# A shorter lead of the first attention in a ring of softmax tiles

## The chip, the cores and the metric

One core of a Trainium2 chip runs the kernel. The metric is the device time in microseconds; the kernel was run several times, and the median counts. TensorE (PE) multiplies matrices, VectorE (DVE) and ScalarE (ACT) do the elementwise work and empty the accumulation banks, GpSimd (POOL) takes a few elementwise steps, and SyncE (SP) issues the DMAs.

## The reference, cut to what matters

A batch of 16 graphs with 512 nodes and 256 features passes through four layers, all in float32. Each ends in a residual and a norm over the features.

```python
x = layernorm(x + (norm_adj @ (x @ W0) + b0))                     # layer 0
x = layernorm(x + o + ln(o)),   o = softmax(mask(q k^T)) v @ Wproj # layer 1: attention, 8 heads of 32
for _ in range(3):                                                # layer 2: a gated recurrence
    a = adj @ h
    z = sigmoid(W3 [a, a] + U3 h);  r = sigmoid(W4 [a, a] + U3 h)
    h = (1 - z) * h + z * tanh(W5 [a, a] + U5 (r * h))
x = layernorm(x + h)
x = layernorm(x + softmax(q k^T / sqrt(32) + bias(adj)) v @ Wo)     # layer 3: attention, 8 heads of 32
```

Within a batch everything is one chain. Between batches nothing depends on anything.

## The kernel before, in words

Three batches are in flight, each in buffers of its own (`STREAMS = 3`, batch b uses set b % 3). The matrix products are split into a high and a low part and made with three matmuls each (`product`, L1451 to L1453). Every product lands in one of eight accumulation banks, from which ScalarE takes the high part and VectorE the rest.

Both attentions share one ring of softmax tiles. An attention of one batch (a block) is 32 tiles of 128 queries by 512 keys. A tile is one matmul for the scores (L1500), a masked maximum on VectorE (L1224), the exponential on ScalarE (L990), four transposes on TensorE (L1508) and a copy on either engine (L999, L1235). After every eight tiles comes the product with the values (L1523) and a rescaling (L1528, L1004, L1245, L1012, L884). The queries and keys of four heads are copied into one buffer, `stack`, by twelve DMAs (L823), which wait until the earlier tiles of that head have been read. The ring is strictly in order. Its order is `BLOCKS`: the pair (1, b) is the first attention of batch b, here called A(b), and (3, b) is the second, C(b). Before the change it is

A(0) A(1) A(2) C(0) A(3) C(1) A(4) C(2) ... A(15) C(13) C(14) C(15).

Around it each batch has work that is not in the ring. Ahead of A(b) lie the load, scaling, adjacency product, first weights, a norm, transposes (L1491) and q, k, v. Between A(b) and C(b) lie a projection, two norms, three recurrent steps (each with an adjacency product, gates, and transposes of the state, L1561), and q, k, v again. Behind C(b) come a projection, a norm and the store (L804). Batch b + 3 can be loaded (L800) only when batch b has been stored.

The order of all instructions on all engines is made when the kernel is built. `Order` holds the pieces of work in queues, each with an estimated duration and the pieces it waits for, and runs them through a list scheduler: the piece that can start first goes first, and among those that can start at once the one with the longest way to the end. The table `RANK` adds a number in microseconds to that way, by kind of piece. The result is a fixed instruction list for each engine.

```python
late = TO_PE if piece.engines == ("PE",) else 0.0
...
rank = (start, -way[piece.key], took(piece, e))
```

One row buffer holds in turn the row to be added before the first layer (`scale`), `beta` and `bo`; the order of these loads, `ROWS`, is fixed and not changed.

Of the kernel before, what the change touches and what calls it, by code (L numbers as in the profile page):

```python
# [15 lines left out]
STREAMS = 3  # L16
# [60 lines left out]
def nominal(key):  # L77
# [21 lines left out]
    else:  # L99
# [3 lines left out]

RANK = {"act a": 6.5, "act ax": 3, "act hT": 6.5, "act hf": -5.5, "act k": 0.5, "act n0": -8, "act n1": -4,
        "act n3": -4, "act out0": 0.5, "act out2": 0.5, "act q": -7, "act r": -8, "act rh": 13, "act rows2": -12,
        "act state": 4, "act x3T": 8, "act z": 4, "act zt": 1, "dve a": 1, "dve h": -12, "dve hT": 0.5,
        "dve norm_o": 4.5, "dve out1": -1, "dve proj1": 1, "dve proj3": 6, "dve q": -6, "dve res2": -2,
        "dve rh": -13, "dve rows2": -1, "dve scale": 3, "dve w0": -3, "dve x1T": -8, "dve x2T": -2, "dve x3T": -2.5,  # L110
        "first ax 1": -100, "first ax 2": 298, "first beta": 200, "first k": 3, "first load": 300, "first q": 33,
        "first scale 0": -10, "first scale 1": -3, "first scale 2": 0.5, "first v": -12, "first w0 0": 301,
# [3 lines left out]
        "pool oadd": 2, "pool out3": 0.5, "pool rstd": 3.5, "pool scale": -4, "prep adj0": 100, "prep adj2": -100,  # L116
        "prep bo": 10, "prep deg": -30, "prep dinv": 3, "prep hi_k3": 2, "prep hi_o1": 3, "prep hi_o3": -1.5,
        "prep hi_v3": 10, "prep lo_k3": -1, "prep lo_o1": 7, "prep lo_qkv1": -300, "prep lo_u5": 10,
        "prep lo_w3": -10, "prep mask1": -0.5, "prep mask3": -300, "prep q1": -110, "prep w4": 110,
        "prep w4-w3": -30, "prep w5": 308, "prep warm": 300, "pt": -2, "raw": 1.5, "recip": -2.5, "row": -0.5}  # L120


FIRST = ("scale", "ax", "w0", "n0", "rstd", "x1T", "q", "k", "v", "beta")
# [2 lines left out]
def kind_of(key):  # L126

    kind, what = key[:2]
    if kind == "prep":
        return f"prep {key[2]}"  # L130
    if kind in ("pe", "act", "dve", "pool"):
        b = key[2]
        if what in FIRST and b < STREAMS and (what not in ("q", "k", "v") or key[3] == 1) and (
                what != "rstd" or key[3] == "n0"):
            return f"first {what} {b}" if what in ("scale", "ax", "w0") else f"first {what}"
        return f"{kind} {what}"
    if kind == "load" and what < STREAMS:
        return "first load"
    return f"values {key[2]}" if kind == "values" else kind
# [11 lines left out]
class Order:  # L151
# [31 lines left out]
    def run(self):  # L183
        way = {key: us + RANK.get(kind_of(key), 0.0) for key, us in self.ways().items()}
        done, taken = {}, {}
# [43 lines left out]
def adj_resnorm_kernel(nc, x, adj, w0, b0, wqkv, wproj, bproj, gamma, beta, w3, w3b, u3, u3b, w4, w4b,  # L229
                       w5, w5b, u5, u5b, wq, bq, wk, bk, wv, bv, wo, bo, out):  # L230
    B, N, D = x.shape
# [15 lines left out]
    bs = range(B)  # L247


    BLOCKS = [(1, b) for b in bs if b < STREAMS]  # L250
    for b in bs:
        BLOCKS += [(3, b)] + ([(1, b + STREAMS)] if b + STREAMS < B else [])
    block_at = {block: i for i, block in enumerate(BLOCKS)}


# [6 lines left out]
    def tile_of(t):  # L262

        i, r = divmod(t, TILES)
        gh, r = divmod(r, GROUP)
        h, q = divmod(r, QT)
        return *BLOCKS[i], gh // HALVES, gh % HALVES, h, q

# [61 lines left out]
    for b in bs:  # L330
        j = b % STREAMS
        pe, act, dve, pool, sp = ((e, j) for e in ("pe", "act", "dve", "pool", "sp"))
# [23 lines left out]
        for layer in (1, 3):  # L356
# [75 lines left out]
            row = "beta" if layer == 1 else "bo"  # L432
            add(pool, "POOL", ("pool", row, b), ("dve",) + xT + (FT - 1,), ("row", row_at[row, b]))
            for g in range(G):
# [4 lines left out]
                first = (block_at[layer, b] * TILES + g * HALVES * GROUP)  # L439
# [16 lines left out]

    for t in range(len(BLOCKS) * TILES):
        layer, b, g, half, h, q = tile_of(t)
# [35 lines left out]
    with ExitStack() as ctx:  # L494
        def sb(name, shape, dt=F32):
            return ctx.enter_context(nc.sbuf_tensor(name, shape, dt))

        def sem(name):
            return ctx.enter_context(nc.semaphore(name))
# [6 lines left out]
        mask1 = sb("mask1", [P, NT, N], BF16)  # L506
        mask3 = sb("mask3", [P, NT, N])
# [6 lines left out]
        def of_few(n):  # L514
            nonlocal taken
            taken += n
            return few[:, taken - n:taken]

        cols = of_few(5 * FT).rearrange("p (i f) -> p i f", i=5)
        dinv, power, least, one, spare = (of_few(n) for n in (NT, NT, P_RING, 1, SPARE))  # L520
# [23 lines left out]
        stack = sb("stack", [P, 2, HG, N], F32R)  # L544
# [7 lines left out]
        rsum = o32[:, :].rearrange("p (q c) -> p q c", q=QT)  # L552
# [11 lines left out]
        raw = nc.alloc_sbuf_tensor_at("raw", [P, FT, PLAIN], F32, offset=at)  # L564
# [9 lines left out]
        deg = probs[:, 2, 0:3 * NT].rearrange("p (i t) -> p i t", i=3)  # L574
# [41 lines left out]
        def signals(name, steps):  # L616
            return [Signal(sem(f"{name}{j}"), steps) for j in js]
# [21 lines left out]
        state = signals("state", ["x2_0", "x2_1"])  # L639
# [7 lines left out]
        summed = signals("summed", [f"{n}{t}" for n in ("n0", "n1", "n2", "n3") for t in range(NT)])  # L647
        ALL = range(len(BLOCKS) * TILES)
        groups = range(len(BLOCKS) * GROUPS)
        shifted = Signal(sem("shifted"), ALL)  # L650
# [993 lines left out]
```

How the kernel before makes its waits and increments, by code:

```python
        def wait_free(pe, *name):  # L695
            uses = order.on_bank[order.banks[name]]
            n = uses.index(name)
            if n and uses[n - 1] != ("warm", 0):
                sig, value = last_read(*uses[n - 1])
                pe.wait_ge(sig.sem, value)
# [11 lines left out]
        def wait_full(eng, *name):  # L714
            bank_full = full[order.banks[name]]
            eng.wait_ge(bank_full.sem, bank_full.at(name))
# [1 line left out]
        def wait_sig(eng, sig, step, b):  # L719
            eng.wait_ge(sig.sem, sig.at(step, b // STREAMS))
# [1 line left out]
        def wait_pt(eng, t):  # L722
            for sig, mine in ((pt_act, moved["ACT"]), (pt_dve, moved["DVE"])):
                last = max([u for u in mine if u <= t], default=None)
                if last is not None:
                    eng.wait_ge(sig.sem, sig.at(last))
# [24 lines left out]
            def raw_loads(what):  # L752
# [12 lines left out]
                        sp.dma_start(to, w.rearrange("(o p) c -> p o c", p=P)).then_inc(gru_loaded, 16)  # L765
                elif what == "rows":
                    for i, v in enumerate((gamma, bproj)):
                        sp.dma_start(rows[:, 1 + i, :], v.partition_broadcast(P)).then_inc(rows_loaded, 16)
                elif what == "bo_sum":
                    sp.wait_ge(prep_dve.sem, prep_dve.at("bo"))
                    sp.dma_start(bo_sum[:, :], raw_bo[0:1, :]).then_inc(bo_stored, 16)
                else:
# [64 lines left out]
            def bias_columns():  # L837
                pool.wait_ge(rows_loaded, 16 * 2)
                pool.wait_ge(small_loaded, SMALL)
```

## Time and profile before

| | us |
|---|---|
| median of 3 runs | 2557.17 |
| lowest and highest | 2555.69, 2558.51 |
| span of the profiled execution | 2555.1 |
| TensorE busy in it | 2518.8 |
| ScalarE busy | 1935.7 |
| VectorE busy | 1872.5 |
| GpSimd busy | 757.7 |

The span runs from the first to the last instruction of one profiled execution; for that execution no time of its own is given beside the span, so it is set against the median, which lies 2.1 us above. Busy time is the time in which an engine had an instruction in work. The ends of matmuls are modelled, so a busy TensorE is not yet a TensorE at its peak.

### The profile page before, as it was taken

What the parts mean: (1) busy time and instruction counts of PE and PEld (TensorE: products, weight loads), DVE (VectorE), ACT (ScalarE), POOL (GpSimd) and SP (SyncE); (2) the same over time, 40 slices, a digit from 0 to 9 for tenths busy, and PEclk for the clock granted to TensorE, in tenths of its full rate; (3) what the DMA queues carried; (4) which work ended last, traced back from release to release, by engine and by line L of the source; (5) the groups of instructions that cost most, each with busy time, mean ns of one, the idle gap of its engine ahead of it and who ended that gap; (6) DMA issues with size and microseconds to landing.
All of it is one profiled execution on the core that took longest, in us unless ns stands there. A gap on an engine that the chain in (4) does not pass through costs nothing.

```text
span 2555.1 us, 50270 instructions
## 1 busy us (share of the span) xinstructions
PE 2518.8 (99%) x17401; PEld 2043.1 (80%) x17401; DVE 1872.5 (73%) x5440; ACT 1935.7 (76%) x4388; POOL 757.7 (30%) x1083
## 2 busy tenths in 40 slices
PE   8999999999999999999999999999999999999997
PEld 6777787888878888888888888888888888778875
DVE  8858848778686786867768587685877868666776
ACT  5858849678596886959869597785968869675787
POOL 2223332323224232242332324232232322423222
PEclk9999999999999999999999999999999999999999
DMA  5302113022130312203122131221303123021122
GB/s 145 78 19 59 26 46 71 26 61 45 46 77 20 76 30 59 65 21 77 43 54 53 41 70 32 54 51 46 78 19 67 38 54 70 20 52 27 28 54 69
DMA packets 91083, 132.15 MB, mean 52 GB/s; under 512 B 15921, under 2 KB 40146, under 8 KB 90834
## 3 DMA queue, kind: packets, MB, share of 16 engines
q1 hardware_dynamic: 90834, 128.94, 21.4%
q8 instruction: 143, 2.34, 0.4%
q14 instruction: 106, 0.87, 0.1%
HBM read 19.83 MB, written 8.39 MB: 11 GB/s over the span
## 4 chain that ended last, share of the span: by engine, by line
PE 91%; ACT 3%; DVE 3%; issue 1%; SPq 1%; POOL 1%; DMA 0%; ACTq 0%; POOLq 0%; DVEq 0%
PE bank L1451 18%; PE bank L1453 18%; PE bank L1452 18%; PE bank L1508 16%; PE bank L1523 9%; PE bank L1500 8%; PE bank L1528 2%; PE bank L1491 2%; PE bank L1561 1%; ACT probs L990 1%; ACT PT L999 1%; DVE gate L1209 0%; ACT res L1027 0%; SPq L749 0%; DVE probs L1224 0%
## 5 line engine op out<-in xcount | busy, mean ns | idle before, releaser
L990 ACT ACTIVATE probs<-probs,few 128x512 f32<-128x512 f32 x1024 | 732.0, 722 | 38.9 <-DVE few L1224 36.5
L1224 DVE CUSTOM_DVE_ANT_0 probs<-bank,mask 128x512 f32<-128x512 f32 x1024 | 675.4, 685 | 111.8 <-PE bank L1508 65.2
L1508 PE MATMUL bank<-ident,probs 128*128 128x128 f32 x4096 | 580.5, 273 | 7.0 <-ACT probs L990 5.9
L1508 PEld LDWEIGHTS bank<-ident,probs 128*128 128x128 f32 x4096 | 485.4, 141 | 76.6 <-issue 10.3
L999 ACT ACTIVATE PT<-bank 128x512 f32<-128x512 f32 x672 | 377.7, 594 | 51.9 <-PE bank L1528 42.8
L1500 PE MATMUL bank<-stack 96*128 96x512 f32 x1024 | 411.6, 450 | 1.0 <-DVE few L1224 0.8
L1235 DVE COPY PT<-bank 128x512 f32<-128x512 f32 x352 | 240.7, 687 | 69.5 <-PE bank L1528 48.2
L1451 PE MATMUL bank<-feat,W 128*128 128x512 f32 x640 | 258.6, 404 | 0.0
L884 POOL TENSOR_TENSOR feat<-o,feat 128x256 fp32r<-128x256 f32 x128 | 95.2, 743 | 542.0 <-ACT feat L1012 541.5
L1453 PE MATMUL bank<-feat,W 128*128 128x512 f32 x640 | 252.7, 395 | 0.0
L1452 PE MATMUL bank<-feat,W 128*128 128x512 f32 x640 | 252.7, 395 | 0.0
L1523 PE MATMUL bank<-PT,vh 128*32 128x256 f32 x4096 | 250.5, 382 | 0.3 <-DVE few L1224 0.3
L1451 PE MATMUL bank<-qk,W 128*128 128x512 f32 x576 | 231.8, 402 | 0.0
L1453 PE MATMUL bank<-qk,W 128*128 128x512 f32 x576 | 227.5, 395 | 0.0
L1452 PE MATMUL bank<-qk,W 128*128 128x512 f32 x576 | 227.4, 395 | 0.0
L1027 ACT ACTIVATE res<-res,few 128x256 f32<-128x256 f32 x256 | 139.7, 595 | 95.0 <-POOL few L869 92.8
L1451 PE MATMUL bank<-adjT,qk 128*128 128x512 f32 x512 | 204.6, 400 | 5.3 <-DVE qk L1374 2.4
L911 POOL TENSOR_TENSOR o<-sums,few 128x256 f32<-128x256 f32 x128 | 82.2, 642 | 412.0 <-DVE sums L1240 411.6
L1523 PEld LDWEIGHTS bank<-PT,vh 128*32 128x32 f32 x4096 | 118.6, 109 | 106.0 <-issue 35.9
L1452 PE MATMUL bank<-adjT,qk 128*128 128x512 f32 x512 | 202.4, 395 | 0.0
L1453 PE MATMUL bank<-adjT,qk 128*128 128x512 f32 x512 | 202.0, 395 | 0.0
L990 ACT ACTIVATION_READ_ACCUMULATOR probs<-probs,few 128x1 f32 x1024 | 201.8, 197 | 0.0
(113 smaller groups left out, 4972.7 us busy)
## 6 DMA issues: line engine op xcount, KB each, us to landing
stack<-qk SPq DMA_DIRECT2D x768, 128.0 KB, 2.4
res<-in_x_dram SPq DMA_DIRECT2D x16, 512.0 KB, 3.8
out_dram<-res SPq DMA_DIRECT2D x16, 512.0 KB, 3.0
rows<-bo_sum SPq DMA_DIRECT2D x15, 128.0 KB, 2.9
rows<-in_L_gnn_bias_dram SPq DMA_DIRECT2D x14, 128.0 KB, 2.9
rows<-in_L_gnn_ln_beta_dram SPq DMA_DIRECT2D x14, 128.0 KB, 2.9
PT<-in_adj_dram SPq DMA_DIRECT2D x1, 1024.0 KB, 5.3
vh<-in_L_gnn_w_w_dram SPq DMA_DIRECT2D x2, 512.0 KB, 9.3
```

The source lines that it names most:

```text
L884: i = pool.tensor_tensor(feat[j][:, LO, gh // HALVES, sl], o32[:, :], feat[j][:, HI, gh // HALVES, sl].bitcast(F32), ALU.subtract)
L990: k = act.activation(p, p, ACT.Exp, bias=least[:, t % P_RING:t % P_RING + 1], scale=-1.0, accum_out=sums[:, grp % 2, q * HG + h:q * HG + h ...
L999: k = act.activation(PT[:, t % PT_RING, :], place("transpose", t)[:, :], ACT.Copy)
L1027: k = act.activation(res[j][:, t, :], res[j][:, t, :], ACT.Identity, bias=mv[j][:, t, 0:1], scale=mv[j][:, t, 1:2])
L1224: k = dve.tensor_tensor_reduce(out=probs[:, t % P_RING, :], in0=place("scores", t)[:, :], in1=mask[:, half * QT + q, :], scale=1.0, scalar ...
L1235: k = dve.tensor_copy(PT[:, t % PT_RING, :], place("transpose", t)[:, :])
L1451: pe.matmul(dst, a(HI), b(LO), start=start, stop=False)
L1452: pe.matmul(dst, a(HI), b(HI), start=False, stop=False)
L1453: return pe.matmul(dst, a(LO), b(HI), start=False, stop=stop)
L1500: k = pe.matmul(place("scores", t)[:, :], stack[0:STACKED * HD, 0, h, cs], stack[0:STACKED * HD, 1, h, :], start=True, stop=True)
L1508: k = pe.transpose(place("transpose", t)[:, m * P:(m + 1) * P], probs[:, t % P_RING, m * P:(m + 1) * P], ident[:, :])
L1523: pe.matmul(dst[h * HD:(h + 1) * HD, 0:QH], v_v[j][:, m, c:c + HD], pt_v[:, pt_slots(grp, h), m, :], start=(m == 0), stop=(m == NT - 1))
```

## The change

The lead of the first attention falls from three batches to two: `BLOCKS` starts with A(0) A(1), and A(b + 2) follows C(b). The ring becomes

A(0) A(1) C(0) A(2) C(1) A(3) C(2) ... C(13) A(15) C(14) C(15).

The number of buffer sets stays three. The `RANK` table is replaced as a whole by another one with more entries; all else is the same. The diff, with the two tables cut:

```diff
-RANK = {"act a": 6.5, "act ax": 3, "act hT": 6.5, "act hf": -5.5, "act k": 0.5, "act n0": -8, "act n1": -4,
...
-        "pe hT": 20, "pe proj1": -3.5, "pe q": 0.5, "pe r": -0.5, "pe v": 3.5, "pe w0": 5, "pe x1T": -1.5,
...
+RANK = {"act ax": 80.53, "act c": 10.01, "act hT": 5.52, "act hf": -0.19, "act k": 2.4, "act n0": -11.72,
...
+        "pe cw": 4, "pe hT": 118.66, "pe k": -0.65, "pe proj1": 1.49, "pe proj3": -51.87, "pe q": -0.97, "pe r": -1.23,
+        "pe v": 3.24, "pe w0": 9.96, "pe x1T": 16.3, "pe x2T": -5.31, "pe x3T": 49.73, "pe z": 6.71, "pe zu": 2.75,
...
@@ -247,9 +255,10 @@
-    BLOCKS = [(1, b) for b in bs if b < STREAMS]
+    LEAD = STREAMS - 1
+    BLOCKS = [(1, b) for b in bs if b < LEAD]
     for b in bs:
-        BLOCKS += [(3, b)] + ([(1, b + STREAMS)] if b + STREAMS < B else [])
+        BLOCKS += [(3, b)] + ([(1, b + LEAD)] if b + LEAD < B else [])
```

## Rows read from the trace of the kernel before

**Rows 1.** The page: span, busy times of TensorE and weight loads, granted clock.

```profile
span 2555.1 us, 50270 instructions
...
PE 2518.8 (99%) x17401; PEld 2043.1 (80%) x17401; DVE 1872.5 (73%) x5440; ACT 1935.7 (76%) x4388; POOL 757.7 (30%) x1083
...
PEclk9999999999999999999999999999999999999999
```

**Rows 2.** Windows of one period: length, busy (x instructions) by engine, clock, DMA.

```profile
844.30:1000.00 155.70, 155.70 (x1085) 127.24 (x1084) 114.49 (x337) 120.44 (x275) 47.47 (x68) 1.00 0.22 51
1000.00:1155.70 155.70, 155.70 (x1085) 127.24 (x1084) 114.51 (x337) 120.44 (x275) 47.47 (x68) 1.00 0.22 51
```

**Rows 3.** Timeline of TensorE, undisturbed matmuls: start us, us, what.

```profile
647.70 0.40 PE L1451 MATMUL bank<-adjT,qk 128*128 128x512 f32 x1
...
650.27 0.40 PE L1453 MATMUL bank<-feat,W 128*128 128x512 f32 x1
...
2494.55 0.28 PE L1451 MATMUL bank<-W,feat 128*128 128x256 f32 x1
...
2495.85 0.28 PE L1453 MATMUL bank<-W,feat 128*128 128x256 f32 x1
```

**Rows 4.** Groups by line and shape: count, busy us, mean ns, idle before.

```profile
L1508 PE MATMUL bank<-ident,probs 128*128 128x128 f32 x4096 | 580.5, 273 | 7.0 <-ACT probs L990 5.9 <-ACT PT L999 0.3
...
L1451 PE MATMUL bank<-feat,W 128*128 128x512 f32 x640 | 258.6, 404 | 0.0
```

**Rows 5.** Timeline of TensorE: first and last tiles of blocks, state transposes.

```profile
93.42 0.48 PE L1500 MATMUL bank<-stack 96*128 96x512 f32 x1
...
221.41 1.04 PE L1561 MATMUL bank<-ident,vh 128*128 128x128 f32 x8
...
251.15 0.48 PE L1500 MATMUL bank<-stack 96*128 96x512 f32 x1
...
2284.54 0.71 PE L1500 MATMUL bank<-stack 96*128 96x512 f32 x2
...
2494.24 0.48 PE L1500 MATMUL bank<-stack 96*128 96x512 f32 x1
```

**Rows 6.** The chain that ended last: start us, us, piece.

```profile
549.19 1.86 PE bank L1523 x32
```

**Rows 7.** Windows of five stretches that make up the span.

```profile
0.00:40.00 40.00, 28.49 (x151) 24.12 (x152) 28.86 (x58) 21.70 (x40) 5.93 (x22) 0.96 0.62 188
40.00:400.00 360.00, 352.57 (x2396) 282.27 (x2395) 264.64 (x770) 264.06 (x600) 102.30 (x145) 1.00 0.22 49
400.00:2160.00 1760.00, 1759.95 (x12306) 1436.83 (x12305) 1296.04 (x3818) 1370.91 (x3127) 534.72 (x753) 1.00 0.22 51
2160.00:2500.00 340.00, 337.41 (x2185) 271.02 (x2184) 247.08 (x671) 240.26 (x528) 103.20 (x138) 1.00 0.17 41
2500.00:2555.10 55.10, 40.33 (x370) 28.87 (x368) 35.90 (x126) 38.76 (x98) 11.54 (x26) 0.97 0.19 49
```

**Rows 8.** Windows of one period's two parts: ring stopped, ring running.

```profile
621.40:688.50 67.10, 67.10 (x361) 55.06 (x360) 39.01 (x110) 36.40 (x70) 27.53 (x41) 1.00 0.12 33
688.50:777.00 88.50, 88.50 (x726) 72.14 (x725) 75.40 (x227) 83.95 (x206) 19.93 (x27) 1.00 0.29 65
```

**Rows 9.** Timeline of SyncE's queue between C(3) and A(6).

```profile
801.49 0.40 SPq L804 DMA_DIRECT2D out_dram<-res  x1
804.45 0.39 SPq L800 DMA_DIRECT2D res<-in_x_dram  x1
...
838.87 31.78 SPq L823 DMA_DIRECT2D stack<-qk  x24
```

**Rows 10.** Timeline of SyncE's queue near the end.

```profile
2464.45 27.48 SPq L823 DMA_DIRECT2D stack<-qk  x15
2491.97 0.59 SPq L804 DMA_DIRECT2D out_dram<-res  x1
```

More of the change, by code:

```diff
@@ L101, in nominal @@
     return us, LATE[kind]
-RANK = {"act a": 6.5, "act ax": 3, "act hT": 6.5, "act hf": -5.5, "act k": 0.5, "act n0": -8, "act n1": -4,
[L107 to L112, printed above, removed]
[3 rows of a table removed]
[L116 to L120, printed above, removed]
@@ new lines @@
+RANK = {"act ax": 80.53, "act c": 10.01, "act hT": 5.52, "act hf": -0.19, "act k": 2.4, "act n0": -11.72,
+        "act n1": 26.1, "act n2": 1.88, "act n3": -27.67, "act out0": 1.14, "act out2": 0.5, "act q": -18.92,
+        "act r": 5.4, "act rh": -9.54, "act rows2": 12.64, "act scale": -0.21, "act state": -5.81, "act v": 5.6,
+        "act x1T": 5.97, "act x2T": 2.67, "act x3T": 1.55, "act z": 1.36, "act zt": -14.35, "dve a": 8.23,
+        "dve ax": -0.46, "dve b0": 16.03, "dve h": -14.81, "dve hT": 4.98, "dve k": -30.26, "dve mom_o": 10.49,
+        "dve out1": -1.32, "dve proj1": 26.19, "dve proj3": -0.12, "dve q": 14.8, "dve r": -15.19, "dve res2": -1.03,
+        "dve rh": -1.94, "dve rows2": 299.23, "dve scale": 0.86, "dve w0": -64.59, "dve x1T": -0.49, "dve x2T": -0.47,
+        "dve x3T": -2.78, "exp": -0.82, "first ax 0": 4.53, "first ax 1": 0.41, "first ax 2": -1.68, "first beta": 0.5,
+        "first k": -3.16, "first load": -1.87, "first n0": -17.72, "first q": -3.4, "first rstd": 204.33,
+        "first scale 0": -8.87, "first scale 1": -7.77, "first scale 2": 8.51, "first v": -24, "first w0 0": 4.76,
[3 rows of a table added]
+        "pool beta": -20.25, "pool bo": 1.74, "pool hf": -25.07, "pool oadd": -1.43, "pool out3": -491.55,
+        "pool rh": 188.64, "pool rstd": 276.57, "pool scale": 241.79, "prep adj0": -31.1, "prep adj1": -23.61,
+        "prep adj3": 6.65, "prep bo": 2.82, "prep cols": 46.18, "prep deg": 214.04, "prep dinv": 12.04,
[3 rows of a table added]
+        "prep lo_w0": 0.73, "prep mask1": 0.88, "prep mask3": 16.77, "prep pow": -27.3, "prep q1": 4.3,
+        "prep q3": 2.94, "prep u3": -19.58, "prep u5": -53.35, "prep w3": 3.79, "prep w4": -4.86, "prep w4-w3": 25.81,
+        "prep w5": 13.69, "prep warm": -15.96, "pt": -2, "raw": 5.98, "recip": -5.82, "row": -0.08, "rsum": 118.21,
+        "stack": -16.09, "store": 1.05, "stt": 0.43, "values 0": 236.49, "values 1": 5.38}
```

6 rows, old and new, of the table RANK are left out of this document.

## Prediction

> **What bounds the kernel now.** I read the page first: TensorE is busy for 99% of the span, and the granted clock is full throughout [rows 1]; VectorE and ScalarE are busy for about three quarters [rows 2]. A busy TensorE need not be a full one, since the ends of its matmuls are modelled, so the second view is the cadence. Where nothing interrupts, the 512-column matmul starts every 0.2336 us (eleven steps in 2.57 us) and the 256-column one every 0.118 us (eleven in 1.30 us) [rows 3]. Eight transposes that last 1.04 us, each 0.273 us long, start (1.04 - 0.273) / 7 = 0.110 us apart [rows 4, 5], and the 32 matmuls of a values group take 1.86 us of the chain [rows 6].
>
> With the counts this gives TensorE's work for one of the 16 batches. There are 5184 matmuls with 512 columns outside the ring (nine groups, 640, 576 and 512 times three), so 324 x 0.2336 = 75.7; 1920 with 256 columns (three groups of 640), so 120 x 0.118 = 14.2; 64 scores x 0.2336 = 14.9; transposes (4096 of the ring and 1024 others) 320 x 0.109 = 34.9; eight values groups x 1.86 = 14.9, and about 0.15 each for entering and leaving that shape = 1.2. The sum is 155.8 us.
>
> The third view is the period. Two successive stretches of 155.7 us hold the same 1085 matmuls, and the busy times of every engine repeat within 0.1 us [rows 2]. So in the middle the kernel is TensorE's work and nothing else: 155.7 measured against 155.8 summed. VectorE takes 114.5 and ScalarE 120.4 of each period.
>
> What is left is at the two ends. 16 x 155.7 = 2491.2, and the span is 2555.1: 63.9 us. TensorE is idle for 11.5 in the first 40 us and for 14.8 in the last 55, for 7.4 and 2.6 in the stretches beside these, and for 0.05 in the 1760 us between [rows 7]. The rest is preparation (up to 10 us of matmuls, nearly all in the first 40 us) and waits so short that the modelled ends cover them. I take 63.9 - 10 - 11.5 - 14.8 = about 27 us as what an order of the work could still win, all of it between 40 and 400 us and after 2160 us. The first 11.5 are loads and preparation, and the last 14.8 the tiles of the last block, which alternate between engines, and the closing norm and store.
>
> **The change, part by part.** No instruction is added or removed: the ring still has 1024 tiles. What changes is which tiles neighbour each other.
>
> *The middle.* Call A(b) the first attention of batch b and C(b) its second. Before, A(b + 3) stands straight behind C(b), in the same buffers, so the ring stops while the output of b is projected and stored, batch b + 3 loaded and its first matmuls made: 67.1 us per period in which TensorE runs full on the recurrent steps (361 matmuls, 67.10 busy of 67.10) [rows 8]. The store, load and stack DMAs show this chain: store at 801.5, load at 804.5, stack from 838.9 [rows 9]. After, two blocks stand between C(b) and A(b + 3), so this chain is covered. The stop was costing nothing, for TensorE was full in it; removing it gains 0, because the 155.7 us of TensorE's work remain.
>
> The price is a shorter cover for the other chain, from A(b) to C(b), with three recurrent steps. Before, four blocks and two stops lay over it; after, two blocks. Its shortest passage in this trace is batch 0: the first tile of A(1), 93.4, to the first of C(0), 251.2: 158 us [rows 5]. The ring's own pace is some 42 us a block (88.5 us for two with their neighbours [rows 8]). In the new order a period lasts at least half of (this chain plus two blocks): (158 + 85) / 2 = 122 us. That is below 155.7, so TensorE stays the bound until the chain has grown to 226 us. Both ends: 0 if it stays below, and for each 10 us beyond, 5 us a period over some 13 periods. I take 0, since the traffic that lengthens the chain is matmul work that has to be done anyway.
>
> *The start.* Until C(0) can begin, the new order has only A(1) to run in the ring. A block costs TensorE 32 x (0.2336 + 4 x 0.109) + 4 x 2.2 = 30.3 us; the work between A and C is 155.7 - 60.6 - 17.7 (adjacency, first weights, q, k, v) - 2.8 (last projection) = 74.6. Over the 158 us there are A(1) with 30.3, batch 0 with 74.6, and batch 1 from 133 us on, 118 / 158 of 74.6 = 55: 160 us, just enough and with no reserve. Before, A(2) was in reserve too. Bounds: a gain up to the 7.4 us that the busy time shows idle here [rows 7] and the hidden part, a loss of as much.
>
> *The end.* The new ring closes A(15), C(14), C(15), the old one A(15), C(13), C(14), C(15). The chain from A(15)'s last tile (2284.5) to C(15)'s first (2494.2) took 210 us before [rows 5], with two blocks over it. If it shrinks to 158, the filling is C(14) with 30.3, batch 15 with 74.6, two projections with 5.7, and what is left of batch 14: that must be 48 us or more of its 74.6. If it is, nothing is lost; if 20 are left, 28 us stand idle.
>
> *The ranks.* They decide ties between ready pieces, on all queues, the preparation included. They can't touch the middle's sum, only the 27 us. I take about a third of those, 8 us: more seems too much, with fewer streams to fill the ends from, and less too little, since the old start is visibly loose [rows 7].
>
> *SyncE's queue.* Before, store and load fell into the ring's stop, where no stack copy was due [rows 9]. After, they stand among the stack copies of A(b + 2), on one queue, in order; a store that waits for the last norm holds them up. The only place of the old trace with this crossing is the tail, 15 stack copies over 27.5 us and a store behind them [rows 10]; in the 340 us that hold it TensorE is idle for 2.6 [rows 7]. From both sides: 0, or 1 us a period. I take 0, and keep 13 us for the range.
>
> The sum: 2555.1 + 0 (middle) - 8 (ends) = 2547.1. The median lies 2.1 us above the span, so **2549 us**.
>
> One rule of the Trainium skill speaks for far more (Perfetto Trace Analysis, "Optimization Strategy" and "Identifying the Most-Contended Engine"): where the contended engine changes between regimes, interleaving them can help, and TensorE's headroom is to be judged by LDWEIGHTS busy and not by matmul busy. Here LDWEIGHTS is busy for 80% [rows 1], which by that rule would leave a fifth; the rows on the cadence disagree.
>
> **The rivals.**
> 1. *The ends come out even*: what the ranks win, the thinner filling takes. 2552 to 2562, 2557.
> 2. *The ends get longer (the other side)*: less than 40 us of batch 14 is left when A(15) ends, or the 160 us at the start don't mesh. Price: some 20 us of the tail's 28, less the ranks' 8, so 12 more: 2569. For it: the filling was computed at no reserve. Against it: the planner prefers the longest way, so it puts off batch 14 for A(15).
> 3. *The queue or the chain costs something in every period*: 1 us x 13 = 13: 2570; a chain of 240 us instead of 226 would cost 7 x 13 = 91: 2648, which I leave outside.
> 4. *TensorE is not full in the ring's stretch*, and spreading the ring shortens the period: 5 us of hidden waiting in 88.5 would give 13 x 5 = 65, so 2492. For it: ScalarE is busy for 84 of these 88.5 us and for 36 of the stop's 67.1 [rows 8]. Against it: the cadence sum leaves no 5 us. This is what the skill's rule would make of it.
>
> **How the numbers follow.** Forecast 0.41, even 0.25, longer ends 0.19, every period 0.12, TensorE not full 0.03. The measurement can tell 0.2%, 5 us, from no change. Faster: 0.41 + 0.03 = 0.44; same 0.25; slower 0.19 + 0.12 = 0.31. The range goes from 2535 (22 of the 27 us won) to 2580 (the longer ends at their full 28 us, less some of the 8); the forecast case alone spans 2537 to 2552.
>
> **What would show it.** Right: periods in the middle of 155.7 us again, with TensorE full and with the scores spread over them; C(0) near 250 us; an idle sum outside the middle that is 8 us lower. Wrong: a middle period of over 156.5 us, waits of the scores for the stack copies, or over 15 us idle between the end of A(15) and C(15).

## The result, and the profile after

The change made the kernel slower: a median of 2615.66 us (2615.04 to 2616.76, 4 runs) against 2556.48 before (2555.69 to 2558.51, now 4 runs too), a ratio of 1.0232 with a 95% interval of 1.0217 to 1.0246. That is 59 us more. The forecast was 2549, and the range ended at 2580.

The page of the changed kernel: span, busy times, the chain by engine.

```profile
span 2614.9 us, 50087 instructions
...
PE 2546.4 (97%) x17401; PEld 2055.3 (79%) x17401; DVE 1900.9 (73%) x5457; ACT 1951.7 (75%) x4385; POOL 747.1 (29%) x1083
...
PE 84%; DVE 8%; ACT 3%; POOL 2%; issue 1%; SPq 1%; DMA 0%; DVEq 0%; ACTq 0%; POOLq 0%
```

Against [rows 1] TensorE makes the same 17401 matmuls in 27.6 us more of busy time and stands idle for 68.5 us where it was 36.3. Part of the longer busy time is the granted clock: it is at its lower level for 45 us in all, against 7 us before. By the pace of the rows at the end of this document (0.213 us instead of 0.117 between two matmuls) that is 17 us of the 59 at most, an estimate. (All line numbers after are higher by nine: the scores are L1509, the ring's transposes L1517.)

Windows of the changed kernel: the first 40 us, the stretch to the first tile of C(2), the ten periods from there to the first tile of C(12), the end.

```profile
0.00:40.00 40.00, 23.86 (x117) 19.19 (x118) 28.49 (x56) 21.72 (x40) 7.37 (x22) 0.89 0.60 188
40.00:570.40 530.40, 517.68 (x3441) 419.24 (x3440) 380.79 (x1086) 378.91 (x844) 149.24 (x217) 0.98 0.19 44
570.40:2164.40 1594.00, 1573.56 (x10842) 1272.90 (x10841) 1173.32 (x3379) 1214.07 (x2734) 469.92 (x671) 1.00 0.21 50
2164.40:2614.90 450.50, 431.29 (x3007) 343.97 (x3005) 318.31 (x939) 336.97 (x771) 120.58 (x175) 0.99 0.21 48
```

The middle is where the time went. Ten periods took 1594.0 us, 159.4 each, against 155.7 in [rows 2], with 20.4 us of idle TensorE where [rows 7] show 0.05 in 1760. That is 37 us in ten of the sixteen periods; of the 17 that are not idle time some 3 are the clock's, by the estimate above, and the rest is in waits that the modelled ends of matmuls cover, which no view separates. The rest of the 59 came ahead of this stretch and behind it; the first 40 us alone lose 4.6 us more than before.

The ring still stops, but once in two batches: four blocks, then a stop. Timeline of TensorE, the scores that open C(2), close A(4) and open C(4); then windows of the four blocks and of the stop behind them.

```profile
570.45 0.94 PE L1509 MATMUL bank<-stack 96*128 96x512 f32 x3
...
689.50 0.48 PE L1509 MATMUL bank<-stack 96*128 96x512 f32 x1
...
888.67 0.94 PE L1509 MATMUL bank<-stack 96*128 96x512 f32 x3
```

```profile
570.30:818.70 248.40, 246.37 (x1798) 198.63 (x1797) 184.59 (x552) 203.69 (x475) 65.34 (x86) 1.00 0.24 55
818.70:888.60 69.90, 67.79 (x375) 55.43 (x375) 49.69 (x126) 39.48 (x75) 28.82 (x49) 1.00 0.13 33
```

C(2) opens at 570.4, A(4) ends at 689.5, and C(4) opens at 888.7: two blocks take 119 us, the chain from A(4) to C(4) 199, and together they are the 318 us of two periods. In the stop TensorE idles for 2.1 us, and in the four blocks ahead of it for 2.0; in [rows 8] it did in neither. The longest waits of TensorE in the ten periods (us in total, times, longest):

```profile
PE bank L1500 <- ACT res L1036: 8.0, 15, 1.2
PE bank L1532 <- DVE PT L1244: 4.1, 5, 0.8
PE bank L1517 <- ACT probs L999: 3.8, 5, 0.8
```

The first is in the stop, the other two belong to the ring's own tiles and make up as much. I followed the first; its timeline, of TensorE first:

```profile
852.22 0.73 PE L1500 MATMUL bank<-ident,res 128*128 128x128 f32 x2 [0.26 <-ACT res L1036]
854.12 0.33 PE L1500 MATMUL bank<-ident,res 128*128 128x128 f32 x1 [1.18 <-ACT res L1036]
854.62 0.77 PE L1500 MATMUL bank<-ident,res 128*128 128x128 f32 x5 [0.16 <-ACT res L1036]
```

These are the transposes x2T of batch 5. They wait for the last norm behind the first attention, and everything behind them in TensorE's fixed list waits too. Why that norm is late is seen on VectorE and GpSimd, a few us earlier:

```profile
841.26 3.00 POOL L885 TENSOR_TENSOR res<-res,vh 128x512 f32<-128x512 f32 x2
841.41 3.40 DVE L1335 SCALAR_TENSOR_TENSOR gate<-gate,vh 128x512 f32<-128x512 f32 x2
844.22 3.18 POOL L910 TENSOR_TENSOR feat<-gate,feat 128x512 fp32r<-128x512 f32 x2
844.73 2.95 DVE L1309 SCALAR_TENSOR_TENSOR vh<-vh,few,rows 128x256 f32<-128x256 f32 x2
```

The two operations of L1335 take 1.7 us each where their group's median is 0.68, the two of L1309 1.5 instead of 0.48. In the whole trace 13 of the 96 operations of L1335 and 29 of the 64 of L1309 are lengthened by over 15%, each while GpSimd works on SBUF. Groups of the changed kernel:

```profile
L1335 DVE SCALAR_TENSOR_TENSOR gate<-gate,vh 128x512 f32<-128x512 f32 x96 | 77.5, 819 | 4.8 <-ACT gate L1060 4.8
...
L1309 DVE SCALAR_TENSOR_TENSOR vh<-vh,few,rows 128x256 f32<-128x256 f32 x64 | 52.8, 864 | 6.2 <-POOL res L885 6.2
```

The same two lines before, L1326 and L1300, took 708 and 522 ns on average, so (819 - 708) x 96 + (864 - 522) x 64 = 33 us of VectorE's time are new. The list scheduler has no such lengthening in its durations.

### The profile page after: what moved, and what is told of

It reads as the page before. It is cut to its first block, busy times and chain, and to the rows that moved or that the text cites. A ratio compares the mean times of both kernels' runs of the same rounds, so it can differ in the third digit from the quotient of the medians.

```text
span 2614.9 us, 50087 instructions
## 1 busy us (share of the span) xinstructions
PE 2546.4 (97%) x17401; PEld 2055.3 (79%) x17401; DVE 1900.9 (73%) x5457; ACT 1951.7 (75%) x4385; POOL 747.1 (29%) x1083
## 4 chain that ended last, share of the span: by engine, by line
PE 84%; DVE 8%; ACT 3%; POOL 2%; issue 1%; SPq 1%; DMA 0%; DVEq 0%; ACTq 0%; POOLq 0%
PE bank L1460 16%; PE bank L1462 16%; PE bank L1461 16%; PE bank L1517 15%; PE bank L1532 8%; PE bank L1509 8%; DVE vh L1309 2%; PE bank L1537 2%; PE bank L1500 1%; PE bank L1570 1%; DVE gate L1218 1%; ACT probs L999 1%; DVE probs L1233 1%; ACT res L1036 1%; POOL few L870 1%
## 5 line engine op out<-in xcount | busy, mean ns | idle before, releaser
L1517 PE MATMUL bank<-ident,probs 128*128 128x128 f32 x4096 | 590.8, 273 | 19.5 <-ACT probs L999 15.3
L1517 PEld LDWEIGHTS bank<-ident,probs 128*128 128x128 f32 x4096 | 489.9, 141 | 103.5 <-issue 22.3
L1509 PE MATMUL bank<-stack 96*128 96x512 f32 x1024 | 431.9, 460 | 2.9 <-DVE few L1233 1.6
L1008 ACT ACTIVATE PT<-bank 128x512 f32<-128x512 f32 x669 | 384.7, 598 | 63.8 <-PE bank L1517 31.8
L1532 PE MATMUL bank<-PT,vh 128*32 128x256 f32 x4096 | 250.0, 382 | 4.4 <-DVE PT L1244 4.3
L1532 PEld LDWEIGHTS bank<-PT,vh 128*32 128x32 f32 x4096 | 119.5, 109 | 110.8 <-issue 36.8
L910 POOL TENSOR_TENSOR feat<-gate,feat 128x512 fp32r<-128x512 f32 x96 | 127.2, 1340 | 237.1 <-ACT feat L1064 237.1
```

Of the source, the lines that this page charges most:

```text
L910: i = pool.tensor_tensor(feat[j][:, LO, f, :], src[j][:, f, :], feat[j][:, HI, f, :].bitcast(F32), ALU.subtract)
L1008: k = act.activation(PT[:, t % PT_RING, :], place("transpose", t)[:, :], ACT.Copy)
L1509: k = pe.matmul(place("scores", t)[:, :], stack[0:STACKED * HD, 0, h, cs], stack[0:STACKED * HD, 1, h, :], start=True, stop=True)
L1517: k = pe.transpose(place("transpose", t)[:, m * P:(m + 1) * P], probs[:, t % P_RING, m * P:(m + 1) * P], ident[:, :])
L1532: pe.matmul(dst[h * HD:(h + 1) * HD, 0:QH], v_v[j][:, m, c:c + HD], pt_v[:, pt_slots(grp, h), m, :], start=(m == 0), stop=(m == NT - 1))
```

## The experiments

Twelve kernels, each timed beside the kernel before on the same chip. (The changed kernel was not timed again; the kernel before repeats within 0.5 us from chip to chip.) Two theories stood at first: the ring's order costs the time, or the new rank table does.

**The order alone**, with the old table:

```diff
-RANK = {"act ax": 80.53, "act c": 10.01, ...
+RANK = {"act a": 6.5, "act ax": 3, ...
```

> The new ring order with the old rank table. Theory O (the order costs the time: the chain from A(b) to C(b) has two blocks over it instead of four, so that in the ring's stops too little matmul work is ready): at least as slow as the changed kernel, 2610 to 2660 us, with TensorE idle in every period of the middle. Theory R (the new ranks cost the time): back near 2557 us, 2550 to 2570.

Measured 2737.98 us, ratio 1.0707 (1.0691 to 1.0723). Two periods of the middle take 337.7 us. The largest single wait comes six times, 36.6 us in all: w0 of a coming batch (here 8) stands in TensorE's list where its input isn't ready. One row of the timeline:

```profile
1219.21 0.55 PE L1452 MATMUL bank<-W,feat 128*128 128x256 f32 x1 [6.10 <-DVE feat L1200]
```

**The table alone**, on the old order:

```diff
-    BLOCKS = [(1, b) for b in bs if b < LEAD]
+    BLOCKS = [(1, b) for b in bs if b < STREAMS]
```

> The old ring order with the new rank table. Theory O: middle periods stay near 155.7 us with TensorE full; only the start keeps the 8 us that the changed kernel lost in its first 40 us, so 2560 to 2575 us. Theory R: 2600 us or more, with the middle period near 159 us.

Measured 2622.13 us, 1.0256 (1.024 to 1.0271), with middle periods of 159.6 us:

```profile
873.70:1033.30 159.60, 157.86 (x1087) 127.57 (x1086) 119.42 (x344) 119.10 (x272) 47.42 (x67) 1.00 0.21 50
```

So each half of the change is slow with the other half missing, and neither theory stands as put: theory R named this time and period but failed on the first kernel; theory O held there, beyond its range, and failed here. With the new table a period takes about 159.5 us in either order; with the old table it takes 155.7 in the old order and 168.9 in the new. These two kernels don't say, then, what the order costs with a good table of its own. That question stayed for the last pair.

**One piece later in TensorE's list:**

```diff
+    for b in bs:
+        late = [("pe", "x2T", b, f) for f in range(FT)]
+        i = line.index(late[0])
+        if line[i:i + 4] == late + [("pe", "w0", b + 1, tp) for tp in range(NT // 2)]:
+            line[i:i + 4] = line[i + 2:i + 4] + late
```

> The changed kernel, but on TensorE alone the two x2T pieces of every second batch stand behind the two w0 pieces of the next batch instead of ahead of them (six places). Theory O: the adjacency product behind them waits for rows2 all the same, at the end of the same chain of norms, so the idle time only moves: within 4 us of the changed kernel. Rival P (a bad place of one piece in TensorE's list): the wait of 2.6 us disappears in six places, and three drops of the clock with it: 12 to 20 us faster.

Measured 2615.33 us (2611.1 to 2616.55), as before the edit. The wait moved to w0 and to the adjacency product behind it:

```profile
851.74 0.36 PE L1467 MATMUL bank<-W,feat 128*128 128x256 f32 x1 [1.95 <-DVE feat L1215]
...
856.43 0.47 PE L1467 MATMUL bank<-adjT,qk 128*128 128x512 f32 x1 [0.77 <-DVE qk L1328]
```

At 852 us neither of the two pieces next in the list was ready: the list runs short of ready work there, and exchanging them doesn't mend that.

**GpSimd's addition cut** to 8 of 256 columns, all lists as they are:

```diff
-                i = pool.tensor_tensor(res[j][:, sl, :], res[j][:, sl, :], v_v[j][:, sl, :], ALU.add)
+                i = pool.tensor_tensor(res[j][:, sl, 0:8], res[j][:, sl, 0:8], v_v[j][:, sl, 0:8], ALU.add)
```

> The changed kernel, with GpSimd's addition of the attention output (L885) cut to 8 of 256 columns, so that most of the first attention's residual is left out of the sum. Orders of all engines stay. If VectorE's operations are stretched because GpSimd works on SBUF beside them, the two operations of norm_o that start with it (L1309) fall from 0.86 us on average to under 0.7, x2T comes 1.5 to 2.5 us earlier in every second period, and 8 to 18 us are won. If they are long for another reason: L1309 stays at 0.86 us and the time within 5 us.

Measured 2588.19 us, 1.0124 (1.0107 to 1.014): 27 us of the 59 are gone, more than expected. L1335 is back at its median, L1309 fell to 730 ns, not under 700: 20 of its 64 operations are still lengthened, most of them by L910. TensorE's waits for x2T in ten periods fall from 8.0 us to 0.8, its idle time there from 20.4 to 9.7. It is also at the lower clock for 21 us in all instead of 45; by the same estimate, up to 11 of the 27 us are the clock's. Window of two periods, now 315.2 us:

```profile
561.30:876.50 315.20, 313.36 (x2172) 253.94 (x2170) 231.30 (x676) 243.44 (x549) 89.64 (x135) 1.00 0.22 50
```

**The addition moved to VectorE**, nothing left out:

```diff
+            pools.remove(("pool", "oadd", b, tp))
+            line.insert(line.index(("dve", "mom_o", b, tp)) + 1, ("dve", "oadd", b, tp))
...
-                i = pool.tensor_tensor(res[j][:, sl, :], res[j][:, sl, :], v_v[j][:, sl, :], ALU.add)
+                i = dve.tensor_tensor(res[j][:, sl, :], res[j][:, sl, :], v_v[j][:, sl, :], ALU.add)
```

> The changed kernel with the addition of the attention output (32 instructions of 1.4 us on GpSimd, L885) moved to VectorE behind the moments of the same rows; all other pieces keep their places in every engine's list. Theory G (GpSimd's work beside VectorE stretches VectorE's operations and the chain of norms with them): VectorE gets 32 x 0.7 = 22 us more work and still the kernel is 8 to 25 us faster than the changed one, 2590 to 2607 us, and the stretched L1309 falls below 0.75 us. Rival V (VectorE's load decides, and the earlier gain came from work left out): no faster than 2612 us.

Measured 2599.65 us, 1.0167 (1.0152 to 1.0183): 16 us faster than the changed kernel, with more work on VectorE. L1309 (L1313 here) is at 630 ns. The same move in the kernel before:

> The same move in the kernel before, whose lists hardly let GpSimd's operations meet VectorE's (the operations in question take 0.52 us there, against 0.86). Theory G: nothing to win, within 4 us of 2557. If the move is good in itself, whatever the order: 8 us or more faster.

Measured 2556.83 us, 0.9998 (0.9989 to 1.0007), no difference. In the kernel before, where few operations were lengthened, the move is worth nothing.

**Both of GpSimd's operations cut**, the addition and the low part of the state:

```diff
-                i = pool.tensor_tensor(feat[j][:, LO, f, :], src[j][:, f, :], feat[j][:, HI, f, :].bitcast(F32),
-                                       ALU.subtract)
+                i = pool.tensor_tensor(feat[j][:, LO, f, 0:8], src[j][:, f, 0:8], feat[j][:, HI, f, 0:8].bitcast(F32),
+                                       ALU.subtract)
```

> The changed kernel with two of GpSimd's operations cut to 8 columns, the addition of the attention output and the low part of the recurrent state (L910), so that most of the first attention's residual and most low parts of the recurrence are left out. It shows what the order costs without any meeting of the two engines. Theory G alone: the middle period returns to 155.7 to 156.3 us and the time to 2565 to 2575. Theory G plus O (the order also leaves too little ready work when the ring's copies wait behind norm work on VectorE and ScalarE): a middle period of 157 us or more and 2575 to 2590.

Measured 2580.17 us, 1.0092 (1.0075 to 1.0109). L1309 is at 533 ns, as in the kernel before, and GpSimd has 13 us less per period to do; still two periods take 313.8 us, 156.9 each, and not 155.7. No wait for x2T is left in ten of these periods; the 4.1 us in which TensorE waits for copies of the ring's tiles (L1532) are there as before.

```profile
557.70:871.50 313.80, 312.67 (x2172) 253.85 (x2169) 229.28 (x676) 243.00 (x548) 68.12 (x135) 1.00 0.22 51
```

**The start.** The old table's entries for preparation and first pieces in the new table:

> The changed kernel with the old rank table's entries for the preparation and the first pieces (all names that begin with prep, first or raw), the rest of the table new. If the preparation's order costs the 8 us that TensorE lost in its first 40 us: 12 to 14 us idle there instead of 21.5, and the kernel 5 to 10 us faster, 2606 to 2611, as long as what follows isn't upset by the shift. If the rank entries are only good together: no faster, or slower.

Measured 2614.24 us, 1.0223 (1.0208 to 1.0238). TensorE is busy for 29.54 us of the first 40 instead of 23.86, and no more than 1.4 us of it reach the end, less than the two medians can tell apart; 5 to 10 were expected:

```profile
0.00:40.00 40.00, 29.54 (x154) 25.21 (x155) 29.23 (x59) 22.26 (x42) 6.21 (x22) 0.96 0.60 188
```

**GpSimd's addition three times over**, in both kernels, to see which of them bears a longer chain:

```diff
-                i = pool.tensor_tensor(res[j][:, sl, :], res[j][:, sl, :], v_v[j][:, sl, :], ALU.add)
+                for op, name in ((ALU.add, "a"), (ALU.subtract, "b"), (ALU.add, "c")):
+                    i = pool.tensor_tensor(res[j][:, sl, :], res[j][:, sl, :], v_v[j][:, sl, :], op)
```

> The kernel before, with GpSimd's addition of the attention output done as add, subtract, add in turn (5.6 us more of GpSimd per batch, and as much longer a chain of norms). Theory C (what makes the new order slow is that the chain from A(b) to C(b) has no slack left, so that each stretch of it reaches TensorE): here four blocks lie over the chain, and the cost is at most 1 us a batch, 2557 to 2573 us. Rival (meetings of VectorE and GpSimd cost TensorE time wherever they stand): 2 us a batch or more, over 2589.

> The same in the changed kernel. Theory C: most of the 5.6 us of each batch and of the meetings it adds reach TensorE, which waits in its fixed order: 3 to 7 us a batch, 2665 to 2730 us. Rival: as much as in the kernel before, whatever that is.

Measured 2623.62 us (1.0263, 1.0248 to 1.0279) in the kernel before and 2692.28 (1.0528, 1.0511 to 1.0546) in the changed one: 67 and 77 us more. The expectation for the kernel before was wrong, the one for the changed kernel held. But the longest wait on TensorE in the kernel before, in the waits by engine and line (us in total, times, longest), is not for the norms:

```profile
PE bank L1533 <- POOL o L916: 27.8, 13, 3.7
```

L916 is the ring's own small GpSimd operation, queued behind the longer additions, and TensorE's values group waits for it. The clock is at its lower level more often as well. The pair lengthened a queue that the ring needs, not only the chain, so it doesn't tell the two apart.

**Both orders with the same treatment.** The planner was told of the meetings, and a random search over the ranks, from each order's own table, minimised the planned span; the old order was given less time for it.

```diff
             clock[e] = start + took(piece, e)
+            if piece.key[1] in MET and e == "DVE":
+                clock[e] += min(MET[piece.key[1]], 0.65 * max(0.0, clock.get("POOL", 0.0) - start))
```

> The new ring order. The planner adds up to 2.0 us to norm_o and up to 1.1 us to rh on VectorE when GpSimd is at work as they start, and the ranks were searched again with that. If the loss came from meetings that the planner didn't know of: 20 to 35 us faster than the changed kernel, 2580 to 2595, with L1309's mean under 0.7 us or its length allowed for. If a better table can bring the order to the old time: under 2565. If the plan's own idle time and the start weigh as much as the meetings: 2590 to 2605.

> The old ring order with the same planner, ranks searched in the same way from the old table, for less time. If the order of the ring is what leaves too little ready work: near the kernel before or a little faster, 2545 to 2562 us, and 25 us or more faster than the new order with the same treatment. If the treatment decides and not the order: within 10 us of it.

Measured: the new order 2615.25 us (1.0236, 1.0219 to 1.0253), the old order 2556.36 (1.0002, 0.9993 to 1.0011). The treatment gave neither of them anything, and the 59 us between the orders stayed; for the new order none of the three expectations came true, the old order came out as its first one had it. The useful part is the traces. Groups of the kernel with the old order, the lines that stand for L1335 and L1309 and one that was hardly stretched before, L1326; then one of its periods:

```profile
L1326 DVE SCALAR_TENSOR_TENSOR gate<-gate 128x512 f32<-128x512 f32 x96 | 93.0, 969 | 3.3
L1317 DVE SCALAR_TENSOR_TENSOR gate<-gate,vh 128x512 f32<-128x512 f32 x96 | 69.0, 733 | 6.0 <-ACT gate L1042 6.0
...
L1291 DVE SCALAR_TENSOR_TENSOR vh<-vh,few,rows 128x256 f32<-128x256 f32 x64 | 35.1, 589 | 8.3 <-POOL res L867 8.3
```

```profile
844.70:1000.50 155.80, 155.80 (x1085) 127.64 (x1084) 120.22 (x342) 119.02 (x270) 47.19 (x68) 1.00 0.22 51
```

VectorE is busy for 120.2 us of this period, 5.7 more than in [rows 2], and TensorE is full all the same. Of the 5.7, 3.4 are five more copies of ring tiles, which VectorE took over from ScalarE, and 2.9 are lengthened operations (2.4 of them L1326; other lines are a little shorter). Over the whole kernel the lengthening sums to 48 us here, to 40 in the changed kernel and to 8 in the kernel before. So as much of it as the new order has costs the old order nothing, though it falls on other operations: most of it on the gates of the recurrence here, most on the norm behind the first attention there. In the new order, searched again, L1309 (L1292 there) still takes 964 ns, and TensorE waits 19.0 us in six places for a low part from GpSimd:

```profile
PE bank L1443 <- POOL feat L893: 19.0, 6, 3.2
```

## Why the prediction was wrong, step by step

**What bounds the kernel** was right: the cadence sum gave 155.8 us of matmul work per batch, and the best any run reached is 155.7 to 155.8. A faster period, rival 4, never appeared.

**The middle is the step that failed**: "I take 0, since the traffic that lengthens the chain is matmul work that has to be done anyway". The term of the middle was 0 and measured 3.7 us a period: TensorE does wait there, 2.0 us a period by the idle time alone, and not for matmul work but for norms and tile copies of VectorE and ScalarE that come late in its fixed list. The relation that I tested it with could not have shown this. Its terms were taken from places without the traffic: the chain takes 199 us, not 158, and the two blocks 119, not 85, so the threshold for the chain was not 226 us but 192. Half of 199 + 119 is 159, but that proves nothing: since C(b + 2) opens at the end of both, their sum is two periods whatever makes them long, a full TensorE included. By length that is rival 3, which I had priced at 1 us a period and given 0.12; its other form, a chain that costs several us in every period, I left outside.

**Which delays make the chain long** I hadn't asked. I took that matmul work alone would lengthen it. The runs show VectorE and GpSimd meeting: 27 us of the 59 go with one GpSimd operation, 35 with two (shown by the cuts, which also take GpSimd's own time out of the chain, a share the runs don't separate, and give back some of the clock; 16 us come back when the addition is merely moved). What is left at 156.9 us a period, some 1.2 a period more than before, isn't attributed piece by piece. That in one stop the two pieces next in TensorE's list are both late is shown by exchanging them without effect.

**The stop "was costing nothing"**: right, but I drew too little from it. Nor was it removed: it comes once in two periods. With four blocks and two stops over it the old chain never held TensorE up in the middle, and the last pair shows that this cover absorbs about 3 us of lengthened VectorE operations per period. I take it that this cover is what the change gave away. It isn't shown apart from the table: the cover alone doesn't help, since the old order with the new table has periods of 159.6 us, and that no table brings the new order back to 155.7 was tried with one search only.

**The ranks "can't touch the middle's sum, only the 27 us"**: a second step that failed, in both of its halves. With the other order's table the middle period went to 159.6 (old order) and 168.9 (new order). Wins of the ranks at the ends did not come: the first 40 us lost 4.6, and mending them gave 1.4 at most.

**The start and the end**: C(0) opened at 254.6 against 251.15 [rows 5], as computed from the filling. From the last tile of A(15), 2388.4, to the first of C(15), 2552.2, passed 164 us, near the 158 that I took as the shortest; TensorE idled for 3 us in it, not for over 15; the end was not the place of the loss.

**SyncE's queue**: the crossing came (a store at 688.2 us between stack copies), and the scores waited for the copies for 0.9 us in all. Zero was right.

## What to carry to other kernels

An engine that is full in a pause of another pipeline shows that the pause is free, but not that it can be removed: the pause may be the cover that absorbs late work elsewhere. Before shortening the distance between two stages, ask which pieces of the other engines come late behind it: a chain measured in the emptiest place of the trace hides them, and a chain plus its blocks measured after the change is the period by definition. And a list made by a planner is fitted to one order: change the two together, and judge an order only with its own best table on both sides.

## What the runs showed of the hardware

Operations of VectorE with two SBUF operands are lengthened where they meet an operation of GpSimd that reads SBUF: most of those of L1309 and L1335 in the changed kernel took 1.4 to 1.8 us instead of 0.48 (L1309) and 0.68 (L1335). They end 0.28 us (256 columns) or 0.55 us (512 columns) after GpSimd's does, in both kernels and in the last pair. Operations that read one operand from the accumulation banks keep their time beside GpSimd: none of the 96 of L1329 is over 0.70 us, one of them right ahead of the stretched pair. The Trainium skill says so (SBUF — State Buffer, "Who interferes with whom"): a VectorE instruction with two SBUF inputs contends with a GpSimd instruction that reads SBUF, and this contention is an exclusive lock. The trace agrees, by the ends just given. I had not weighed this rule; it speaks against a schedule that lets the two meet on a chain without cover, not against the new order as such.

The granted clock fell to its lower level in places where TensorE had waited in the stop, twice in the ten middle periods too, where [rows 7] show 1.00 before the change. The other three stops of these periods have waits for x2T too and kept the higher level. A window of the changed kernel with waits for x2T of batch 3, and four of the matmuls behind them, two at either level:

```profile
534.00:538.00 4.00, 2.87 (x15) 2.68 (x16) 2.54 (x4) 3.68 (x7) 0.20 (x1) 0.75 0.00 0
```

```profile
536.55 0.42 PE L1462 MATMUL bank<-W,feat 128*128 128x256 f32 x1
536.77 0.41 PE L1460 MATMUL bank<-W,feat 128*128 128x256 f32 x1
...
539.73 0.28 PE L1460 MATMUL bank<-W,feat 128*128 128x256 f32 x1
539.85 0.28 PE L1461 MATMUL bank<-W,feat 128*128 128x256 f32 x1
```

A mean of 0.75 over these 4 us is half of the time at 1.2 GHz. At that level the 256-column matmuls start 0.213 us apart (twelve steps in 2.56 us from 536.55), at the other 0.117; so some waits cost more than their own length.
